# Three of four mask pieces by ScalarE and GpSimd, and new orders of queues and tail, in a graph-attention kernel with layer norm

## The reference

```python
def _L0_gnn_ref(x, spatial_encoding, edge_encoding, Wq, Wk, Wv, Wout):
    n, d = x.shape                    # 2048, 256
    h = Wq.shape[1] // d              # 8
    scale = d ** (-0.5)
    q = (x @ Wq).reshape(h, n, d)
    k = (x @ Wk).reshape(h, n, d)
    v = (x @ Wv).reshape(h, n, d)
    a = jnp.einsum('hnd,hmd->hnm', q, k) * scale
    a = a + spatial_encoding + edge_encoding
    mask = spatial_encoding == 0.0
    a = jnp.where(mask, -1000000.0, a)
    a = jax.nn.softmax(a, axis=-1)
    a = jnp.where(mask, 0.0, a)
    out = jnp.einsum('hnm,hmd->hnd', a, v)
    out = out.transpose(1, 0, 2).reshape(n, h * d)
    return out @ Wout

x = _layernorm(x + _L0_gnn_ref(x, adj, adj, Wq, Wk, Wv, Wout), axis=-1)
```

## Time and profile before

| | us |
|---|---|
| median of 3 runs | 1913.58 |
| lowest and highest | 1906.4, 1914.65 |
| profiled execution, its time | 1908.7 |
| its span | 1907.0 |
| PE busy | 1821.9 |
| DVE, POOL, ACT busy | 1154.3, 973.5, 854.0 |

### The profile page before, as it was taken

One profiled execution on the slowest core, in us unless ns is written; L12 is line 12 of the kernel. 1 busy time (PEld: TensorE's weight loads), 2 busy tenths in 40 slices (PEclk: granted clock), 3 DMA queues, 4 the chain that ended last, 5 costly groups with the idle time before them and its releaser, 6 DMA issues.

```text
span 1907.0 us, 29335 instructions
## 1 busy us (share of the span) xinstructions
PE 1821.9 (96%) x10272; PEld 1589.0 (83%) x10272; DVE 1154.3 (61%) x2330; ACT 854.0 (45%) x1397; POOL 973.5 (51%) x750
## 2 busy tenths in 40 slices
PE   6988769999999999999999999999999999999996
PEld 5877558988888888988889888898888888898885
DVE  5899864565555555565555555556555555555665
ACT  4544334444454445444454444544445444554432
POOL 5666635454554445544464444544445454544443
PEclk9999889999999999999999999999999999999998
DMA  6776756466655665556664666646655566655663
GB/s 214 220 229 196 216 186 183 148 197 188 184 178 158 194 198 180 162 176 190 186 191 140 195 188 192 187 140 198 189 171 174 165 198 194 183 164 153 181 177 94
DMA packets 186994, 345.96 MB, mean 181 GB/s; under 512 B 39392, under 2 KB 96736, under 8 KB 170464
## 3 DMA queue, kind: packets, MB, share of 16 engines
q10 hardware_dynamic: 65280, 184.62, 30.8%
q1 hardware_dynamic: 121568, 159.47, 29.6%
HBM read 190.84 MB, written 18.87 MB: 110 GB/s over the span
## 4 chain that ended last, share of the span: by engine, by line
PE 81%; issue 1%; DVE 1%; ACTq 1%; POOL 1%; DMA 1%; ACT 1%; SPq 0%; DVEq 0%
PE bank L401 31%; PE y_bank L424 20%; PE bank L366 17%; PE y_bank L422 11%; PE y_bank L420 1%; ACTq L561 1%; DVE blocks L638 0%; POOL p_split L472 0%; DMA raw_x<-in_x_dram 0%; ACT p_split L533 0%; DVE y_acc L727 0%; DMA p_turned<-blocks 0%; PE bank L386 0%; ACT t_p L524 0%; POOL m_sb L479 0%
## 5 line engine op out<-in xcount | busy, mean ns | idle before, releaser
L472 POOL TENSOR_TENSOR p_split<-p_turned,p_split 128x512 fp32r<-128x512 f32 x512 | 660.6, 1306 | 661.3 <-ACT p_split L533 660.9
L401 PE MATMUL bank<-k_split,q_split 128*128 128x512 f32 x3072 | 792.6, 393 | 7.1 <-DVE k_split L605 4.7
L424 PE MATMUL y_bank<-v_split,p_split 128*128 128x512 f32 x1920 | 707.2, 401 | 0.0
L401 PEld LDWEIGHTS bank<-k_split,q_split 128*128 128x128 f32 x3072 | 579.3, 189 | 118.8 <-issue 5.3
L422 PE MATMUL y_bank<-v_split,p_split 128*128 128x256 f32 x2048 | 558.7, 283 | 0.0
L618 DVE CUSTOM_DVE_ANT_0 t_p<-bank,m_sb 128x512 f32<-128x512 f32 x512 | 350.3, 687 | 333.1 <-PE bank L401 311.6
L533 ACT ACTIVATE p_split<-p_turned 128x512 fp32r<-128x512 f32 x512 | 305.1, 622 | 294.9 <-POOL p_split L472 140.4
L424 PEld LDWEIGHTS y_bank<-v_split,p_split 128*128 128x128 f32 x1920 | 365.4, 190 | 77.1
L422 PEld LDWEIGHTS y_bank<-v_split,p_split 128*128 128x128 f32 x2048 | 392.5, 192 | 18.8
L524 ACT ACTIVATE t_p<-t_p,small 128x2048 f32<-128x2048 f32 x128 | 256.9, 2007 | 327.9 <-DVE small L630 205.2
L638 DVE STREAM_TRANSPOSE blocks<-t_p 128x2048 f32<-128x2048 f32 x128 | 295.8, 2311 | 174.9 <-ACT t_p L524 131.3
(11 more groups left out here) (45 smaller groups left out, 755.6 us busy)
## 6 DMA issues: line engine op xcount, KB each, us to landing
m_sb<-m_dram ACTq DMA_DIRECT2D x112, 1024.0 KB, 5.1
p_turned<-blocks SPq DMA_DIRECT2D x1024, 64.0 KB, 2.1
p_turned<-blocks ACTq DMA_DIRECT2D x1024, 64.0 KB, 2.3
raw_w<-in_L_gnn_Wk_dram SPq DMA_DIRECT2D x64, 256.0 KB, 3.8
y_acc<-in_adj_dram SPq DMA_DIRECT2D x64, 256.0 KB, 3.3
raw_w<-in_L_gnn_Wq_dram SPq DMA_DIRECT2D x64, 256.0 KB, 3.6
m_dram<-m_sb SPq DMA_DIRECT2D x16, 1024.0 KB, 5.3
raw_w<-in_L_gnn_Wv_dram SPq DMA_DIRECT2D x64, 256.0 KB, 3.7
```

Source lines behind the costliest of these rows:

```text
L401: mm = nc.tensor.matmul(dst[:], q[:, a, k, f * P:(f + 1) * P], k_split[:, kk, k, b * BANK:(b + 1) * BANK], start=(i == 0), stop=(i == len( ...
L424: mm = nc.tensor.matmul(y[:], hi, v_split[:, j].rearrange("p s d -> p (s d)"), start=False, stop=last)
L472: nc.gpsimd.tensor_tensor(lo, p_turned[:, i * BANK:(i + 1) * BANK].rearrange("p (j b) -> p j b", b=QUAD), hi.bitcast(F32), ALU.subtract).t ...
```

## The change

- Pieces 1, 2 and 3 of each tile's mask go by ScalarE and GpSimd, piece 0 by VectorE's join (in tile 0 only piece 2 goes by GpSimd). A third `zero_mark` is for the join.
- The adjacency pieces lie in `blocks[1]`, one place per piece. The turned tile of head 0 then uses `blocks[0]` alone, so `turn` waits for the shuffle of the tile before; from tile 17 on the two take turns as before. The residual is loaded in two steps, in rounds 2 and 6.
- On DVE `build(t + 1, 0)` comes before `turn`, and piece b+1 is built after score b. On ACT and POOL the splits of P come two at a time in parts 0 and 1, ahead of the mask pieces of parts 1, 2, 3; ACT issues its eight transfers in part 2. On SP piece 0 of the adjacency is loaded before the shuffles and the others after them.
- Stores of the mask count on two semaphores, for even and odd tiles.
- Four K blocks come before the first scores, the others a part earlier. The load of x of the next head is issued within round 12. The first normalised part has 13 tiles and is done in round 129, its square root at the end of ACT's round 128.

```diff
-        adj_place = [y_acc[:, Y_MID + 2 * i:Y_MID + 2 * i + 2, :].rearrange("p a d -> p (a d)") for i in range(4)]
+        adj_place = [blocks[1][:, i * BANK:(i + 1) * BANK] for i in range(BANKS)]
+        def turned_place(tau):
+            return blocks[0 if tau <= TILES else tau % 2]
+        def turned_before(tau):
+            return tau - 1 if tau <= TILES else tau - 2 if tau > TILES + 1 else None
+        by_pool, by_dve = {}, {}
+        for a in range(TILES * BANKS):
+            t, q = divmod(a, BANKS)
+            kind = by_pool if q in ((2,) if t == 0 else (1, 2, 3)) else by_dve
+            kind[a] = len(kind) + 1
...
-        FIRST_K = {(0, 0): (2, 3), (0, 1): (4, 5), (0, 2): (6, 7)}
+        FIRST_K = {(0, 0): (4, 5), (0, 1): (6, 7)}
-        START = (("k", 0, 0), ("k", 0, 1), ("q", 0, 0))
+        START = (("k", 0, 0), ("k", 0, 1), ("q", 0, 0), ("k", 0, 2), ("k", 0, 3))
-        EARLY_NORM = TILES - 4
+        EARLY_NORM = TILES - 3
...
+                load_w(2)
+                load_adj(0, 0)
+                load_w(4)
+                load_adj(0, 1)
+                load_w(5)
+                load_adj(0, 2)
+                load_adj(0, 3)
+                load_w(SLOTS + 2)
+                for q in range(BANKS):
+                    load_adj(1, q)
                 load_w(SLOTS + len(START))
+                load_wout(0)
                 for tau in range(ALL + 1):
...
                         store_m(t)
+                        load_adj(t + 2, 0)
...
                         if tau:
                             shuffle(tau - 1, i)
-                        if h == 0:
-                            load_adj((t + 2) * BANKS + i)
+                        if i == 1 and t == LAST_Q and h + 1 < H:
+                            load_x(h + 1)
+                    if h == 0:
+                        for q in range(1, BANKS):
+                            load_adj(t + 2, q)
-                    if t == LAST_Q and h + 1 < H:
-                        load_x(h + 1)
...
-                        if 2 <= tau < ALL + 2:
-                            lo_p(tau - 2, b)
-                        if tau + 1 < TILES and b in (1, 3):
-                            add_adj((t + 1) * BANKS + b - 1)
+                        if 2 <= tau < ALL + 2 and b < 2:
+                            lo_p(tau - 2, 2 * b)
+                            lo_p(tau - 2, 2 * b + 1)
+                        if tau + 1 < TILES and b:
+                            add_adj(t + 1, b)
...
-                    if tau == TILES:
-                        act.wait_ge(m_stored, 16 * TILES)
+                    if tau < TILES + 2:
+                        act.wait_ge(m_stored[tau % 2], 16 * TILES // 2)
...
-                        if 1 <= tau <= ALL and b >= 2:
-                            shuffle(tau - 1, 2 * b - 4)
-                            shuffle(tau - 1, 2 * b - 3)
+                        if 1 <= tau <= ALL and b == 2:
+                            for i in range(QUADS):
+                                shuffle(tau - 1, i)
                     if t == 0 and tau < ALL:
                         hi_wout(h)
-                for part in range(len(NORM_PARTS)):
-                    sqrt_of(part, NORM_PARTS[part])
+                    if tau == ALL:
+                        sqrt_of(0, NORM_PARTS[0])
+                sqrt_of(1, NORM_PARTS[1])
+                sqrt_of(2, NORM_PARTS[2])
...
-                    if tau >= 2:
+                    if tau and turned_before(tau) is not None:
                         for i in range(QUADS):
-                            dve.wait_ge(shuffled[i], 64 * (tau - 1))
+                            dve.wait_ge(shuffled[i], 64 * (turned_before(tau) + 1))
...
+                    mark = zero_mark[q % 2 if a in by_pool else 2]
+                    if t:
+                        dve.wait_ge(counted, t)
+                    if a in by_pool and by_pool[a] > 2:
+                        dve.wait_ge(m_scaled, by_pool[a] - 1)
+                    if a in by_dve and by_dve[a] > 1:
+                        dve.wait_ge(m_by_dve, by_dve[a] - 1)
...
+                    if tau + 1 < TILES:
+                        build(t + 1, 0)
                     if 1 <= tau <= ALL:
                         turn(tau - 1)
...
-                            if tau + 1 < TILES:
-                                build(t + 1, b)
+                            if tau + 1 < TILES and b < BANKS - 1:
+                                build(t + 1, b + 1)
...
                         all_vars(0, NORM_PARTS[0])
+                    if tau == ALL + 1:
                         inverse_std(0, NORM_PARTS[0])
                         normalise(NORM_PARTS[0])
```

More of the change, by code:

```diff
@@ L128, in graph_attention_layernorm @@
         counted, floor_part, floors = sem("counted"), sem("floor_part"), sem("floors")
-        m_stored = sem("m_stored")
+        m_stored = [sem(f"m_stored{i}") for i in range(2)]
         m_loaded = [sem(f"m_loaded{i}") for i in range(2)]
@@ L178, in due @@
                 yield "k", h, c
-            if t % 2 == 0 and t <= LAST_Q and b == (3 if tau == 0 else 1):
+            if t % 2 == 0 and t <= LAST_Q and b == (2 if tau == 0 else 1):
                 yield "q", h, t // 2 + 1
@@ L302, in shuffle @@
                         sp.dma_start(p_turned[quad(j), i * BANK:(i + 1) * BANK],
-                                     blocks[tau % 2][quad(i), j * BANK:(j + 1) * BANK]).then_inc(shuffled[i], 16)
+                                     turned_place(tau)[quad(i), j * BANK:(j + 1) * BANK]).then_inc(shuffled[i], 16)
                 load_x(0)
-                for a in range(BANKS):
-                    load_w(a + 1)
-                    load_adj(a)
+                load_w(2)
[8 more added lines that the diff above has]
+                    load_adj(1, q)
                 load_w(SLOTS + len(START))
+                load_wout(0)
                 for tau in range(ALL + 1):
@@ L343, in _ @@
                 sp.wait_ge(normed, EARLY_NORM)
-                store_out(4, EARLY_NORM // 2)
-                for t in range(EARLY_NORM, TILES):
+                store_out(4, EARLY_OUT // 2)
+                for t in range(EARLY_OUT, TILES):
                     sp.wait_ge(normed, t + 1)
                     sp.dma_start(out_tokens[t % 2][:, t // 2], y_tokens[:, t % 2, t // 2]).then_inc(stored, 16)
-                sp.wait_ge(stored, 16 * (2 * HALVES + TILES - EARLY_NORM))
+                sp.wait_ge(stored, 16 * (2 * HALVES + TILES - EARLY_OUT))
             @block.tensor
@@ L730, in _ @@
                 lo_of(("x", 0))
-                build(0, 0)
-                lo_of(START[0])
-                build(0, 1)
-                lo_of(START[1])
-                build(0, 2)
-                lo_of(START[2])
-                build(0, 3)
+                for q in range(BANKS):
+                    build(0, q)
+                    lo_of(START[q])
+                lo_of(START[BANKS])
                 for tau in range(ALL + LAG + 1):
```

131 lines of the change are left out of this document (58 added, 73 removed).

## The result

| | before | after |
|---|---|---|
| median, lowest to highest, us | 1911.89 (1906.4 to 1914.65) | 1879.56 (1877.31 to 1880.75) |
| span of the profiled execution | 1907.0 | 1877.4 |

The ratio is 0.9833, interval [0.9808, 0.9858]: 32 us, 1.7% faster. I had forecast 1852, and a sum of 58.3 us less: the direction was right, the size was not, and 1879.56 lies above the range of 1834 to 1876.

What follows compares the result with a forecast made beforehand. TensorE was taken to bound heads 1 to 7, but not head 0 or the tail. Terms -6-26.7-15.1-2.5-8=-58.3 us against the profiled 1908.7 gave 1850.4, put at 1852 for scatter; range 1834 to 1876.

Steps and rivals of the forecast that it cites:

- ScalarE's order as the limit of a round: Head 0, rounds 4 to 14: eight transfers queued before the third scaling give 13.7 us a round, ten rounds 137, -26.7.
- the raw_x wait: Up to 290 us: TensorE's 13.6 us wait goes by an earlier load in round 12, counted within the ten rounds.
- the store's 6.09: End of head 0: ScalarE's 6.09 us behind the last mask store goes with two store semaphores, within -15.1.
- rival 3: Later heads: ScalarE's order makes rounds longer than TensorE's 11.2 us; at 12.0 about 1942; chance 0.08.
- rival 1: Head 0 rounds: VectorE sets the pace at 12.4 us, total 1839; chance 0.15 for 1832 to 1842.
- The single turned buffer: Head 0: turning needs the previous tile's transfers landed; nothing at the median, 3.3 us in a tile at most; taken as nothing.
- The start: Before round 4: 4.7 us of waits for K's splits go; tile 0's exponential comes earlier, bounds 0 and 7.5, taken -6.
- The end of head 0: After round 14's exponential: TensorE's fourth K block comes 19.0 us later, before 34.1, so -15.1.
- the ring of six banks: End of head 0: six banks fill in round 15 and give back part of TensorE's lead; otherwise 2.5 us more.
- raw_x in later heads: A later head: TensorE's 2.5 us wait for raw_x goes because the load lands a round early, -2.5.
- Tail: Last tiles: TensorE's wait behind VectorE goes, -5.5, and most of 2.9 after it; bounds 5.5 and 8.4, taken -8.
- Rival 2: Head 0: single turned buffer or tighter queues add 1 us a tile, and the start gives nothing: 1870; chance 0.23.

Runs made afterwards that it cites:

- experiment 4: The kernel after with ScalarE issuing four and SP twelve of a tile's sixteen transfers in head 0: 1861.24 us, ratio 0.9727 to before.
- experiment 6: The kernel after with two turned buffers from tile 5 on and, in head 0, four transfers a tile by ScalarE, twelve by SP: 1856.17 us, ratio 0.9705.
- experiment 3: The kernel after with adjacency in the space of vt_split from tile 5 on, so two turned buffers again: 1872.75 us, ratio 0.9787 to before.
- experiment 1: The kernel after with SP's loads of weights K 6, K 7 and Q 1 ahead of tile 1's adjacency: 1877.52 us, ratio 0.9815 to before.
- experiment 9: The kernel before with the edit of the tail alone: 1906.4 us, ratio 0.9974 to before.
- experiment 2: The kernel after with weights split four ahead of their use, not three, on ScalarE and GpSimd: 1872.70 us, ratio 0.9787 to before.
- experiment 11: The kernel after with K 6, K 7, Q 1 loaded first, two turned buffers, four ScalarE transfers, later weights split four ahead, looser compare waits: 1843.89 us.
- experiment 8: The kernel before with three edits of the change, raw_x within round 12, two store semaphores and the tail: 1887.69 us, ratio 0.9874 to before.
- experiment 10: The kernel after with P's splits one in each part and ScalarE's transfers four and four: 1881.95 us, ratio 0.9845 to before.
- 7: The kernel after with piece 2 of each mask given back to VectorE's join: 1877.68 us, ratio 0.9821 to before.

## Why the prediction was wrong

**What held.** ScalarE's order as the limit of a round (13.91 against 13.7), the raw_x wait mostly gone, the store's 6.09 gone, the tail's wait for VectorE gone, no slowing of later heads by rival 3 beyond a third of a microsecond a head. That rival 1 was not reached for ScalarE's eight transfers is shown by experiment 4 and, with the buffer's share taken off too, by 6. Five terms of the sum missed, by 28.7 us together, every one to the same side.

**The single turned buffer: "I take nothing".** This step failed. I set the median landing, 2.4 us, against the earliest transpose, and asked for nothing beyond. Three things were off. The start of a transpose needs the last of sixteen landings, so the upper end counts, not the median. The landings of ScalarE's transfers became slower with the change: 1.9 to 7.3 us, median 3.2, from 90 to 250 us (before, over the same stretch, 1.9 to 6.2, median 2.4), at a DMA share of 0.77 in place of 0.68. And a late landing isn't absorbed: the whole chain of the round starts from the transpose, and a transpose late by 0.2 us could cost 1.2 by a slow L660. It cost 5.7 us of the 9.1 by which ten rounds missed (experiment 3); the plain round of 13.9 in place of 13.7 is another 2. The last 1.4 was not separated. It is not the slow L660: the ten rounds of experiment 3 have none and still take 1.3 us more than ten of 13.91.

**The start: "I take -6".** This failed. I had named the danger, loads of K behind pieces of adjacency, and gave it no price. Experiment 1 shows it was 3.9 us. The rest went before round 4: E(1) came 2.95 earlier than before (40.38 against 43.33), E(3) 2.4, and the round from E(3) to E(4) took 16.4 (13.8 before), with its transpose held 1.2 us by landings and an L660 of 0.90. The eight issues are in these rounds too: with four, E(1) to E(4) took 49.5 us in place of 55.1 (experiment 4). By the profile of experiment 9, with E(4) at 97.55, the start did give 2 us, so the miss is 4 to 6.

**The end of head 0: -15.1.** This failed by 8.7 us, the largest of the errors beside the rounds. I looked for the limit of TensorE's lead in the ring of six banks and missed the nearer one, the splits of weights. By the trace of after it is nearly all there: 6.39 us without work until that split was done, and then 5.1 us of matmuls at a granted clock of 0.50, of which I estimate that half was lost. By experiment it is less sure. Experiment 2 took 4.1 off the stretch, and TensorE still lost 3.7 there; experiment 11, with weights four ahead as well, took 66.9 us for it where experiment 6 with three took 67.8. What holds the rest stays open.

**raw_x in later heads: -2.5.** This term was read from a single wait. It is gone from after, but the profile of experiment 9, with the same code up to the tail as before, has none either. Later heads did not get shorter, 225.9 against 225.7 on average, because of something that the sum had at nothing. The median later head took 225.6 us in after and 225.5 to 225.8 in every kernel with its order of P's splits and weights three ahead; it took 225.2 in the four with the old order (before, experiments 8, 9 and 10), and 224.6 with weights four ahead (2 and 11). TensorE's wait before a K block at the end of a later head is mostly 0.73 to 0.76 us in after and 0.38 to 0.43 in before and in experiment 10. With weights four ahead it is gone. So a small part of rival 3 came true, 0.34 us a head or some 2.4 in seven, by way of the weights' splits and not of P's.

**Tail: -8.** The mechanism was right and the size nearly so, 6.8, and 6.0 by itself. What I expected back in the last tile of values came only in part: 7.56 against the 5.6 expected, as its first matmuls take 0.43 and 0.21 us where the later ones take 0.24 and 0.12, after a gap of TensorE of 3.22.

**The whole.** Rival 2 had the right mechanism and the right place, a landing wait and a start that gives nothing, at 1870; with the end of head 0 added it would have been 1879. That this meets the measured time is luck in part: the rival had 12 us for its waits, twice the 5.7 measured, and nothing for the plain round or the later heads. Three small edits that the change hardly speaks of are three quarters of its gain (experiment 8), the third piece is worth nothing (7), and what most kept the rest from paying was one row, eight issues of 0.61 us on the engine whose exponential everything waits for (4).

## What to carry to other kernels

If an engine both computes on the critical chain and issues transfers, count each issue as an instruction of that chain, and try moving some, not all: here 8, 12 and 16 of 16 on SP gave 146, 135 and 159 us for ten rounds. When a buffer that was double becomes single, price the wait with the last landing of the group, at the load that the changed kernel will have, and let nothing absorb it if the chain starts there. Before crediting an engine with a lead, list every look-ahead that feeds it (banks, weights loaded, weights split), and take the shortest. And before a wait in one profile goes into a sum, see whether a second profile of the same kernel has it.

## What the runs showed of the hardware

**VectorE held by GpSimd.** L660 works on one element a partition. It starts while GpSimd has four splits under way, each 1.25 us:

```profile
112.29 5.02 POOL L480 TENSOR_TENSOR p_split<-p_turned,p_split 128x512 fp32r<-128x512 f32 x4 [1.03 <-ACT p_split L541]
...
127.38 5.02 POOL L480 TENSOR_TENSOR p_split<-p_turned,p_split 128x512 fp32r<-128x512 f32 x4 [1.00 <-ACT p_split L541]
```

In the first row the third split starts at 114.80 and ends at 116.08. L660 came at 114.92, just behind its start, and ended at 116.10. In the second row the third split starts at 129.89; L660 came at 129.79, just before, and took 0.21. So 0.2 us earlier or later decides over a whole 1 us of the chain. All 128 of L660 in after go by this: each of the 28 that took over 0.3 us ended within 0.03 us of the end of a GpSimd instruction, and none of the 100 others came with more than 0.16 us of one left. The join of mark and adjacency took 2.30 us beside GpSimd's adds; in after, where GpSimd is idle for all or most of the join (they overlap for 0.5 us at most, and in before for 0.95 us or more), it took

```profile
L697 DVE SCALAR_TENSOR_TENSOR m_sb<-zero_mark,blocks x11: 1166/1208/1226, 94.5 to 240.8; 128x512 f32<-128x512 uint8 x11
```

So of the 2.30 about 1.1 went on GpSimd's account, which the profile counts as busy, and VectorE before was less full than 83.33 of 87.63 says. The Trainium skill (SBUF — State Buffer, Who interferes with whom) says that a VectorE instruction with two inputs in SBUF contends with a GpSimd instruction that reads SBUF, and that the ports which the two share are an exclusive lock. The trace agrees in both places: 1.18 us, to the end of a split, against 0.21, and 2.30 against 1.21.

**Starting a transfer.** The median of an issue was 0.61 us on ScalarE and 0.59 on SP, and four fewer of them a tile on ScalarE shortened plain rounds from 13.9 to 12.6. The rule that the prediction weighed, that a start is usually small beside the transfer (the Trainium skill, DMA: Bandwidth & Descriptors, Issuing engines are not separate DMA queues), does not settle the question here: a transfer took 3.2 us to land, but what counted was the time of the issuing engine.

**TensorE after a gap.** Behind the 6.39 us without work at 255.9, twelve matmuls took 2.90 us, and in the tail the first ones behind 3.22 us took 0.43; later both were back at the usual 1.43 for twelve and 0.24 for one. The granted clock from 262 to 266 us is 0.50, which is 1.2 of 2.4 GHz; from 280 to 312 it is 1.00. So each of these gaps cost more than its length.
